# Attention heads of a transformer layer: all four score groups issued first, the memory update last

## The reference

```python
def step(carry, seg):
    mem, z = carry
    q, k, v = seg
    sq = elu(q) + 1.0
    sk = elu(k) + 1.0
    z = z + sk.sum(axis=-2, keepdims=True)
    scores = einsum('bhsd,bhtd->bhst', q, k) * scale
    att_dot = einsum('bhst,bhtv->bhsv', softmax(scores), v)
    att_mem = einsum('bhsd,bhdv->bhsv', sq, mem) / einsum('bhsd,bhdv->bhsv', sq, z)
    mem = mem + einsum('bhsd,bhsv->bhdv', sk, v)
    att = gate * att_mem + (1.0 - gate) * att_dot
    y = att.reshape(B, SEG, H * DV) @ Wout.T
    return ((mem, z), y)
...
x = x + attention(layernorm(x)) + experts(layernorm(x))
```

## Time and profile before

| what | value |
|---|---|
| runs | 3029.23 us median, 3029.08 to 3029.97 |
| the profiled execution | 3030.45 us, of which the span from first to last instruction is 3029.1 us |
| spans of the 8 cores | 3017.1 to 3029.1 us |
| busy share of the span | PE 79%, DVE 28%, ACT 23%, POOL 1% |
| heads of segment 0 (257 to 391 us) | PE busy 65.25 us, ACT 45.93, DVE 51.75 |
| heads of segment 1 (449 to 632 us) | PE busy 67.75 us, ACT 46.81, DVE 98.13 |
| granted TensorE clock | 0.51 among the heads, 1.00 in the projections |

### The profile page before, as it was taken

One profiled execution on the slowest core, in us unless ns is written; L12 is line 12 of the kernel. 1 busy time (PEld: TensorE's weight loads), 2 busy tenths in 40 slices (PEclk: granted clock), 3 DMA queues, 4 the chain that ended last, 5 costly groups with the idle time before them and its releaser, 6 DMA issues.

```text
span 3029.1 us, 34321 instructions; the slowest of 8 cores (3017.1 to 3029.1 us)
## 1 busy us (share of the span) xinstructions
PE 2401.4 (79%) x12560; PEld 1099.6 (36%) x12560; DVE 839.6 (28%) x2611; ACT 681.9 (23%) x1178; POOL 20.2 (1%) x27
## 2 busy tenths in 40 slices
PE   0646483374365349999999999999999999999995
PEld 0213232232232224444444444444444444444442
DVE  2412315524533532212222222222222222222223
ACT  2223332222222223113113113112112112112110
POOL 0000000000000000000000000000000000000000
PEclk9967585585576569999999999999999999999996
DMA  7030000000003003033033033033033033033014
GB/s 175 0 56 15 1 15 1 1 14 1 1 15 56 1 5 53 1 56 56 1 56 56 1 56 56 1 56 56 1 56 56 1 56 56 1 56 56 1 56 167
DMA packets 33508, 107.81 MB, mean 36 GB/s; under 512 B 1200, under 2 KB 1456, under 8 KB 32320
## 3 DMA queue, kind: packets, MB, share of 16 engines
q0 software_dynamic: 25616, 75.56, 14.8%
q1 hardware_dynamic: 7728, 30.05, 3.0%
HBM read 168.59 MB, written 8.39 MB: 58 GB/s over the span
## 4 chain that ended last, share of the span: by engine, by line
PE 77%; DVE 10%; issue 4%; DMA 4%; ACT 4%; DVEq 0%; SPq 0%; ACTq 0%; POOL 0%; POOLq 0%
PE ps_y L782 29%; PE ps_m1a L751 15%; PE ps_m1b L751 15%; PE ps_s L389 6%; PE ps_a L583 3%; PE ps_s L673 2%; DMA x_tm<-x 2%; DVE attpre L612 1%; DVE attpre L622 1%; DVE tmpsb L618 1%; DMA y<-ybuf 1%; PE ps_lg L231 1%; DMA wosb<-wot 1%; DVE skperm L460 1%; ACT elue L458 1%
## 5 line engine op out<-in xcount | busy, mean ns | idle before, releaser
L782 PE MATMUL ps_y<-h1g,w2sb 128*128 128x512 bf16 x4096 | 893.0, 379 | 0.0
L782 PEld LDWEIGHTS ps_y<-h1g,w2sb 128*128 128x128 bf16 x4096 | 398.2, 98 | 482.9 <-issue 7.2
L751 PE MATMUL ps_m1a<-xn_bf,w1sb 128*128 128x512 bf16 x2048 | 497.4, 387 | 2.4 <-PE ps_y L782 0.3
L751 PE MATMUL ps_m1b<-xn_bf,w1sb 128*128 128x512 bf16 x2048 | 492.5, 384 | 0.0
L761 DVE TENSOR_TENSOR h1g<-h1t,gbc 128x512 bf16<-128x512 bf16 x512 | 217.6, 425 | 762.3 <-ACT h1t L758 762.3
L788 DVE TENSOR_TENSOR out_acc<-out_acc,ps_y 128x512 bf16<-128x512 bf16 x256 | 176.0, 687 | 709.4 <-PE ps_y L782 709.4
L758 ACT ACTIVATE h1t<-ps_m1a,b1sb 128x512 bf16<-128x512 f32 x256 | 175.9, 687 | 733.6 <-PE ps_m1a L751 733.6
L751 PEld LDWEIGHTS ps_m1a<-xn_bf,w1sb 128*128 128x128 bf16 x2048 | 201.1, 99 | 257.1 <-issue 26.7
L751 PEld LDWEIGHTS ps_m1b<-xn_bf,w1sb 128*128 128x128 bf16 x2048 | 203.0, 99 | 250.7 <-issue 16.0
L758 ACT ACTIVATE h1t<-ps_m1b,b1sb 128x512 bf16<-128x512 f32 x256 | 175.9, 687 | 276.5 <-PE ps_m1b L751 276.5
L640 PE MATMUL ps_t<-idb,attpre 128*128 128x128 bf16 x128 | 23.8, 288 | 197.5 <-DVE attpre L622 174.7
(11 more groups left out here) (114 smaller groups left out, 1437.4 us busy)
## 6 DMA issues: line engine op xcount, KB each, us to landing
w1sb<-w POOLq DMA_DIRECT2D x8, 4096.0 KB, 27.1
w2sb<-w POOLq DMA_DIRECT2D x8, 4096.0 KB, 27.6
x_tm<-x SPq DMA_DIRECT2D x4, 2048.0 KB, 46.5
y<-ybuf SPq DMA_DIRECT2D x16, 512.0 KB, 2.7
qsw<-qfm SPq DMA_DIRECT2D x8, 512.0 KB, 5.6
x2a<-x SPq DMA_DIRECT2D x1, 4096.0 KB, 14.1
x2b<-x SPq DMA_DIRECT2D x1, 4096.0 KB, 16.8
wqsb<-wqt POOLq DMA_DIRECT2D x1, 2048.0 KB, 20.3
```

Of the source, the lines that this page charges most:

```text
L751: t_mm = em.op("tensor", lambda t, hh=hh, kk=kk, tt=tt, bk=bk: t.matmul(bk[:, :], w1sb[:, kk, 128 * hh:128 * hh + 128], xn_bf[:, kk, SEG * ...
L782: t_mm = em.op("tensor", lambda t, dd=dd, hh=hh, slot=slot, e=e, bk=bk: t.matmul(bk[:, :], w2sb[:, hh, 128 * dd:128 * dd + 128], h1g[:, sl ...
```

## The change

Two things move in the program of a head. First, all four `s_pair` calls are made right after the copies to `kperm` and `vperm`, ahead of both elu steps; before, two were made after the elu steps and two after the memory update. Second, the four matmuls of the memory update are written after the 16 matmuls of the weighted sum instead of before the second two score groups. No instruction is added or removed.

```diff
+            s_pair(0)
+            s_pair(2)
+            s_pair(1)
+            t_qsw_free = s_pair(3)
             t_e0 = em.op("vector", lambda v, par=par: v.tensor_scalar_min(
                 elut[:, par, :], kperm[:, par, :, :], 0.0),
...
-            s_pair(0)
-            t_qsw_free = s_pair(2)
-
...
-            for tc_ in (0, 1, 2, 3):
-                t_memmm = em.op("tensor", lambda t, tc_=tc_, par=par, h=h,
...
-            s_pair(1)
-            s_pair(3)
...
             slot_cons[("ethead", par)] = t_AD
+            for tc_ in (0, 1, 2, 3):
+                t_memmm = em.op("tensor", lambda t, tc_=tc_, par=par, h=h,
...
+                    waits=tmax(t_skp, t_vperm, cons["mem"] if tc_ == 0 else None),
+                    inc="sp" if tc_ == 3 else None)
+            t_mem_upd_last = t_memmm
```

More of the change, by code:

```diff
@@ L454, in build, with s_pair @@
                 continue
+            t_S = {}
+            def s_pair(tc_, h=h, par=par):
+                b = 0 if tc_ < 2 else 64
+                cc4 = (tc_ % 2) * 4
+                bname = "s0" if b == 0 else "s64"
+                bk = ps_s[0] if b == 0 else ps_s[1]
+                rhs_even = qfm if b == 0 else (qfm if _noqsw else qsw)
+                rhs_odd = (qfm if _noqsw else qsw) if b == 0 else qfm
+                em.op("tensor", lambda t, b=b, cc4=cc4, h=h, bk=bk, re_=rhs_even: t.matmul(
+                    bk[:, 0:256], kfm[b:b + 64, h, cc4:cc4 + 4, 0:32], re_[b:b + 64, h, 0:CH, 0:32],
+                    start=True, stop=False, skip_group_check=True),
+                    waits=tmax(t_kev, t_qev, t_qsw, cons[bname]))
+                t_Smm = em.op("tensor", lambda t, b=b, cc4=cc4, h=h, bk=bk, ro=rhs_odd: t.matmul(
+                    bk[:, 256:512], kfm[b:b + 64, h, cc4:cc4 + 4, 0:32], ro[b:b + 64, h, 0:CH, 0:32],
+                    start=False, stop=True, skip_group_check=True), inc="sp")
+                tE = em.op("scalar", lambda a, tc_=tc_, par=par, bk=bk: a.activation(
+                    ethead[:, par, tc_, :], bk[:, :], AF.Exp, scale=0.125),
+                    waits=tmax(t_Smm, slot_cons.get(("ethead", par))), inc="sa")
+                t_S[tc_] = tE
+                cons[bname] = tE
+                return t_Smm
+            s_pair(0)
+            s_pair(2)
+            s_pair(1)
+            t_qsw_free = s_pair(3)
             t_e0 = em.op("vector", lambda v, par=par: v.tensor_scalar_min(
@@ L482, in build @@
                 continue
[L483 to L504, removed]
-            s_pair(0)
-            t_qsw_free = s_pair(2)
             if _alvl < 4:
-                t_att_ev_last = t_S[2]
+                t_att_ev_last = t_S[3]
                 continue
@@ L524, in build @@
                 t_att_ev_last = [("sp", em.cnt["sp"])]
-                s_pair(1); s_pair(3)
                 continue
@@ L589, in build @@
             slot_cons[("ethead", par)] = t_AD
+            for tc_ in (0, 1, 2, 3):
+                t_memmm = em.op("tensor", lambda t, tc_=tc_, par=par, h=h,
+                                fz=(s == 0 and h in (0, 1) and tc_ == 0),
+                                lz=(s == NSEG - 1 and h == H - 1 and tc_ == 3): t.matmul(
+                    _mem_ap(ps_mem, h), skperm[:, par, tc_, :], vperm[:, par, tc_, 0:64],
+                    start=fz, stop=lz, skip_group_check=True),
+                    waits=tmax(t_skp, t_vperm, cons["mem"] if tc_ == 0 else None),
+                    inc="sp" if tc_ == 3 else None)
+            t_mem_upd_last = t_memmm
+            slot_cons[("skperm", par)] = t_memmm
+            slot_cons[("vperm", par)] = t_memmm
+            slot_cons[("sqh", par)] = t_NU if s > 0 else t_sqh
             if _alvl < 7:
```

## The result

The changed kernel takes 3087.89 us (median of 10 runs) against 3029.39 of the kernel before in the same measurement. The ratio is 1.0195, with a 95% interval of 1.0182 to 1.0208: 59 us slower. The forecast was 3088, from a change of +58.4 us. (Some executions of most kernels here come out tens or hundreds of us longer, up to 3396 for the changed one; the ratios leave these out.)

What follows compares the result with a forecast made beforehand. Heads are bound by a chain through three engines. +63.8 us (segments 1 to 3) and -5.4 (segment 0) give +58.4: 3088.9 for the profiled execution, 3087.6 for the median, taken as 3088; range 3066 to 3108.

Steps and rivals of the forecast that it cites:

- What bounds: Heads: each is one chain through three engines, with nothing of one head beside the next; no engine near full.
- Part 1: ScalarE: four score exponentials ahead start the elu exponential of K at 978.86 instead of 976.97, 1.89 us late.
- Part 2: Segments 1 to 3: delay shifts `ghz`, weighted sum shortens from 1.71 to 1.19 us; +1.33 us a head, +63.8 us.
- Part 3: Segment 0, without `ghz`: `rdc` comes 0.34 us earlier a head, -5.4 us over 16 heads.
- Part 4: Memory update behind the weighted sum: 0.42 us on PE while VectorE combines the head; counted as nothing, 27 us if uncovered.
- The slack of 0.04 us: Segments 1 to 3, elu chain: `ghz` could let L571 start at 980.53; score matmuls held it until 980.57.
- Rival (a): Faster: the sum waits for the scores, not the elu chain; every head gains 0.34 us, 22 us in all, 3008; 3%.
- Rival (c): Much slower: the delay passes whole and the sum still takes 1.71 us with all inputs ready; 3122; 6%.
- Rival (d): Smaller loss: the score exponentials' wait for the bank vanishes; +32 us, 3062; 4%.
- Rival (b): Neutral: exponentials run so far beside the transposes that the delay is under 0.6 us; 3030; 2%.

## Why the prediction was right

By its own steps, with the head shown above (start 1014.26):

| step | forecast, us after the head's start | measured |
|---|---|---|
| first score exponential | 0.90 | 0.89 |
| third (group 1) | 2.30 | 2.31 |
| elu exponential of K | 3.28 | 3.29 |
| `ghz` ends | 6.69 | 6.70 |
| its matmul | 6.84 | 6.85 |
| weighted sum starts | 7.00 | 6.99 |
| `rdc` | 8.19 | 8.15 |

- What bounds: right. The heads are one chain with no overlap between them; the stages of projections and experts did not move.
- Part 1, the delay of 1.89 us: measured 3.29 - 1.39 = 1.90. The wait for the bank was taken from segment 0 and fits: 0.81 us of waiting for `ethead` at 1015.89, and 1.42 us from the first exponential to group 1's, where 1.40 was taken. The trace has 1016.57 to 1017.55 for two exponentials, 490 ns each. The Trainium skill's figure ("ScalarE: Activation LUTs", section "What ACT_TABLE_LOAD costs"), 520 ns from one to the next, would by the prediction's estimate have put the elu exponential at 3.35; the measurement decides for the rows.
- Part 2, +1.33 a head and +63.8: the head shown has +1.29, the three stages +63.45. The sum gained 1.71 - 1.16 = 0.55 us where 0.52 was taken. The rest, some 1.5 us, comes from the heads that the row doesn't stand for. In the last eight heads of a segment the reciprocal of z starts 0.45 us after `sqh` and not 0.34, in both kernels. Before, this was hidden, since the sum waited for its last exponentials; in the changed kernel it isn't, and these heads take 12.82 us instead of 11.40, +1.42 each. Against that, two of the first eight, which took 11.51 and 11.56 us before, lose only 1.0 to 1.1.
- Part 3, -5.4: the stage gave -6.86. A later head does what was worked out; the first head of the segment, which was counted like the others, gained more: its transposes to the next head's took 9.52 us before (253.96 to 263.48) and 8.18 after (252.72 to 260.90), 1.34 us instead of 0.34. Its elu exponential of K is late by 1.20 us only (2.48 before and 3.68 after, from the transposes' start), and its sum ran while the granted clock was still 1.00 (252.70 to 258.60; 0.50 behind it): 0.66 us instead of 1.06.
- Part 4, nothing for the memory update behind the sum: right in its place, at 1022.24, while VectorE works. But that the same move, alone, is a gain of 21 us was not seen in the prediction. It was counted only as a cost to bound. The rows had it: the memory update stood ahead of the score matmuls of groups 1 and 3, and the sum waited for the exponentials behind these.
- The slack of 0.04 us, on which the prediction says that the forecast turns: this reading is too narrow, and the sum came out right in spite of it. 0.04 us is what `ghz` had to spare before its matmul L571. But the sum behind L571 then waited for exponentials, so `ghz` had the 0.55 us of part 2 to spare as well, 0.59 in all by this estimate. The last eight heads show it: before, their L571 starts 0.09 us later (5.08 us after the head's start), and `rdc` comes after 6.85 all the same. Part 2 subtracts both, 1.89 - 0.04 - 0.52, and so is right. What had no slack in the kernel before was the elu chain through `sqh`, the memory reads and the late score groups: with two exponentials ahead 0.47 us of delay cost 0.48.
- Rival (a) needed 1.9 us to spare; there were 0.59. Rival (c) is out by the sum's 1.06 us. Rival (d), no wait for the bank, is out by the 0.81 us. Rival (b) would have needed a delay near zero; only one exponential ahead has that.
- The range of 3066 to 3108 is narrower than the bounds that it is said to come from: +0.91 and -0.76 a head give 3061, +1.74 and +0.07 give 3114. This did not matter here.
- The agreement of the totals, 58.4 against 58.5 of the medians, is closer than the terms are, and in that part luck: the stages give +56.6.

## What to carry to other kernels

Where engines take their work strictly in the order written, filling the idle time of one is free only if what is put there ends before the next critical instruction is ready, or if that one has time to spare. Here one exponential of 0.59 us fitted exactly, and two did not. Write each queue in the order in which its inputs become ready, and do it for all engines at once: PE's new order cost 50 us with ScalarE's old one, 59 with its new one, and with the right one it gained 55 (by the lowest times; each with the memory update moved, which alone gives 21). And follow each chain to the instruction whose end counts, not only to the next place where two meet: here two ends met 0.04 us apart ahead of one matmul, while the sum behind it waited half a microsecond for something else. So taking work out of one of the two gained 0.44 us, ten times that slack.

## What the runs showed that was not expected

The memory update took 0.44 us a head off the path when it left, though by the starts of the matmuls around it, it stood for 0.35 (980.02 less 979.67). The timelines of the two heads have the rest. Group 1's first matmul starts 4.03 us after the head's start instead of 4.44, which is even 0.06 ahead of where the memory update had started (4.09), and its second one follows after 0.16 us instead of 0.19 (961.14 behind 960.98, 980.21 behind 980.02): 0.44 together. Why PE takes them up that much sooner was not tried.
